# Attention row sums: which score tiles VectorE adds, and how its first addition is formed

## The reference

```python
q = _split_heads(x @ Wq + bq, h); k = _split_heads(x @ Wk + bk, h); v = _split_heads(x @ Wv + bv, h)
pattern = einsum('bhid,bhjd->bhij', k, q) * scale
prob = softmax(pattern, axis=-2)
out = einsum('bhis,bhid->bhsd', prob, v)
out.transpose(0, 2, 1, 3).reshape(b, s, h * dv) @ Wo + bo
```

## Time and profile before

| | |
|---|---|
| median of 3 runs | 4653.44 us (4646.86 to 4657.02) |
| the profiled execution | 4646.07 us |
| its span, first to last instruction | 4644.1 us |
| granted TensorE clock, mean | 0.977 |
| busy: PE, DVE, ACT, POOL | 4351.6, 3295.5, 2175.5, 2707.8 us |
| VectorE's copies into acc_d (L1178) | 64, median 1004 ns |
| VectorE's additions into acc_d (L1176) | 128, median 1537 ns |
| GpSimd's additions (L770) | 704 and 64 firsts, 2512 and 2386 ns mean |

### The profile page before, as it was taken

How to read it: one execution, slowest core, us unless ns; L and a number is a source line. 1 busy time by engine, 2 the same in 40 slices (tenths; PEclk the granted TensorE clock), 3 DMA queues, 4 the chain that set the end, 5 groups by cost and what they waited for, 6 DMA issues and landing times.

```text
span 4644.1 us, 67290 instructions
## 1 busy us (share of the span) xinstructions
PE 4351.6 (94%) x25496; PEld 2560.7 (55%) x25496; DVE 3295.5 (71%) x4434; ACT 2175.5 (47%) x3523; POOL 2707.8 (58%) x1205
## 2 busy tenths in 40 slices
PE   7999999999999999999999999858999897999898
PEld 5445454554554545545545545426777665777665
DVE  6777877777777777777787787476666455666455
ACT  5445444444444444444444444315666443666442
POOL 2867767667666676676676776804454332454332
PEclk8999999999999999999999999979999998999999
DMA  2000000000000000000000000010000100000001
GB/s 79 6 11 13 8 11 5 16 11 6 11 15 6 11 6 16 11 5 11 15 6 11 13 8 7 1 59 1 1 1 0 38 1 19 1 1 1 1 1 37
DMA packets 81401, 55.73 MB, mean 12 GB/s; under 512 B 48532, under 2 KB 71016, under 8 KB 81128
## 3 DMA queue, kind: packets, MB, share of 16 engines
q1 hardware_dynamic: 81128, 51.92, 4.2%
HBM read 30.66 MB, written 4.19 MB: 8 GB/s over the span
## 4 chain that ended last, share of the span: by engine, by line
PE 44%; POOL 25%; issue 12%; DVE 11%; ACT 7%; POOLq 1%; DMA 1%; SPq 0%; DVEq 0%; ACTq 0%
POOL accp L770 21%; PE psum L1521 8%; PE psum L1533 8%; PE psum L1668 5%; PE psum L1488 4%; PE psum L1798 2%; PE psum L1714 2%; PE psum L1728 2%; ACT lp L967 2%; POOL accp L766 2%; PE psum L1811 2%; DVE accd L1176 2%; PE psum L1465 2%; PE psum L1705 2%; PE psum L1473 1%
## 5 line engine op out<-in xcount | busy, mean ns | idle before, releaser
L770 POOL TENSOR_TENSOR accp<-accp,prob 128x1024 f32<-128x1024 f32 x704 | 1768.6, 2512 | 492.2 <-ACT prob L921 414.2
L921 ACT ACTIVATE prob<-psum 128x1024 f32<-128x1024 f32 x1024 | 1020.5, 1025 | 1462.7 <-PE psum L1521 1374.6
L1153 DVE TENSOR_REDUCE mx<-psum 128x1 f32<-128x512 f32 x1984 | 1277.2, 685 | 347.3 <-PE psum L1488 298.8
L1533 PE MATMUL psum<-prob,vv 128*64 128x512 f32 x4096 | 992.9, 606 | 0.0
L1488 PE MATMUL psum<-kh,qh 64*128 64x512 f32 x2048 | 492.2, 470 | 56.7 <-DVE mx L1153 48.6
L1533 PEld LDWEIGHTS psum<-prob,vv 128*64 128x64 f32 x4096 | 248.6, 136 | 490.1 <-issue 420.4
L787 POOL TENSOR_TENSOR lp<-lp,lrcp 128x1024 f32<-128x1024 f32 x128 | 242.6, 1895 | 451.7 <-DVE lrcp L1293 451.7
L1488 PEld LDWEIGHTS psum<-kh,qh 64*128 64x128 f32 x2048 | 205.0, 184 | 522.9 <-DVE mx L1153 442.2
L1521 PE MATMUL psum<-nm,one 64*128 64x512 f32 x2048 | 429.1, 408 | 14.1 <-ACT prob L921 6.5
L1521 PE MATMUL psum<-qh,kh 64*128 64x512 f32 x2048 | 412.3, 391 | 0.0
L1521 PE MATMUL psum<-qh,kl 64*128 64x512 f32 x2048 | 412.0, 391 | 0.0
(11 more groups left out here) (197 smaller groups left out, 6797.3 us busy)
## 6 DMA issues: line engine op xcount, KB each, us to landing
kl<-kl SPq DMA_DIRECT2D x64, 256.0 KB, 3.8
wqk<-L_attn_Wq SPq DMA_DIRECT2D x64, 64.0 KB, 2.1
rot_l<-const_rot SPq DMA_DIRECT2D x2, 2048.0 KB, 9.0
out<-lpT SPq DMA_DIRECT2D x32, 128.0 KB, 1.7
wqkv_l<-L_ffn_wqkv SPq DMA_DIRECT2D x4, 768.0 KB, 10.4
w_l<-L_ffn_w SPq DMA_DIRECT2D x4, 618.0 KB
wqk<-L_attn_Wk SPq DMA_DIRECT2D x32, 64.0 KB, 2.0
wv_p<-L_attn_Wv SPq DMA_DIRECT2D x16, 128.0 KB, 2.3
```

The lines of the kernel that those rows point to most:

```text
L770: pool.tensor_tensor(acc_p[cp][:], first[:], prob[kt % PRING][:], ALU.add).then_inc(pool_sum, 1)
L921: act.activation(prob[t % PRING][:], psum[:, S_BANK + 2 * (t % 2):S_BANK + 2 * (t % 2) + 2, :].rearrange("p a b -> p (a b)"), ACT.Exp, sca ...
L1153: dve.tensor_reduce(mx4[:, e, qt, c:c + 1], ps, AX_X, ALU.max).then_inc(ring_free, 1)
L1533: mm = pe.matmul(psum[j * DH:(j + 1) * DH, O_BANK, :], vv[:, kt, s * DH:(s + 1) * DH], prob[t % PRING][:, j * T:(j + 1) * T], start=(kt == ...
```

## The change

Each half gets its own set of three tiles for VectorE: tiles 8, 9 and 12 in the first half, 2, 3 and 10 in the second, in place of 3, 7 and 11 in both. The first two of a set are neighbours, and one addition `prob + prob` into `acc_d` takes both; the copy that started `acc_d` is gone. GpSimd still takes 13 tiles and makes 12 additions and one join per half, with other tile numbers. The waits of ScalarE and the counts of the semaphores follow. The places of the maxima are the same.

```diff
-SUM_DVE = (3, 7, 11)
-SUM_POOL = tuple(k for k in range(KT) if k not in SUM_DVE)
+SUM_DVE = ((8, 9, 12), (2, 3, 10))
+SUM_POOL = tuple(tuple(k for k in range(KT) if k not in tiles) for tiles in SUM_DVE)
 JOIN = -1
-POOL_SEQ = SUM_POOL[1:-1] + (JOIN,) + SUM_POOL[-1:]
-POOL_OPS = len(POOL_SEQ)
-DVE_OPS = len(SUM_DVE)
+POOL_SEQ = tuple(tiles[1:-1] + (JOIN,) + tiles[-1:] for tiles in SUM_POOL)
+POOL_OPS = len(POOL_SEQ[0])
+DVE_OPS = len(SUM_DVE[0]) - 1
...
+        def dve_used(cp, kt):
+            return max(SUM_DVE[cp].index(kt), 1)
...
-                    if kt in SUM_DVE:
-                        act.wait_ge(dve_sum, G * (CP * DVE_OPS) + OFF_DVE + cp * DVE_OPS + SUM_DVE.index(kt) + 1)
+                    if kt in SUM_DVE[cp % CP]:
+                        act.wait_ge(dve_sum, G * (CP * DVE_OPS) + OFF_DVE + cp * DVE_OPS + dve_used(cp % CP, kt))
...
             def add_sum(G, cp, j):
-                kt = SUM_DVE[j]
-                dve.wait_ge(exp_done, G * STEPS + cp * KT + kt + 1)
-                if j:
-                    dve.wait_ge(dve_sum, G * (CP * DVE_OPS) + OFF_DVE + cp * DVE_OPS + j)
-                    dve.tensor_tensor(acc_d[cp][:], acc_d[cp][:], prob[kt % PRING][:], ALU.add).then_inc(dve_sum, 1)
-                else:
-                    dve.tensor_copy(acc_d[cp][:], prob[kt % PRING][:]).then_inc(dve_sum, 1)
+                tiles = SUM_DVE[cp]
+                dve.wait_ge(exp_done, G * STEPS + cp * KT + tiles[j] + 1)
+                left = prob[tiles[0] % PRING]
+                if j > 1:
+                    dve.wait_ge(dve_sum, G * (CP * DVE_OPS) + OFF_DVE + cp * DVE_OPS + j - 1)
+                    left = acc_d[cp]
+                dve.tensor_tensor(acc_d[cp][:], left[:], prob[tiles[j] % PRING][:], ALU.add).then_inc(dve_sum, 1)
...
-                            if kt in SUM_DVE:
-                                add_sum(G, cp, SUM_DVE.index(kt))
+                            if kt in SUM_DVE[cp][1:]:
+                                add_sum(G, cp, SUM_DVE[cp].index(kt))
```

More of the change, by code:

```diff
@@ L407, in adaln_block, with pool_used @@
         OFF_S, OFF_POOL, OFF_DVE, OFF_RING = STEPS, CP * POOL_OPS, CP * DVE_OPS, RING_PAIR
-        def pool_used(kt):
-            return 1 if kt == SUM_POOL[0] else POOL_SEQ.index(kt) + 1
+        def pool_used(cp, kt):
+            return 1 if kt == SUM_POOL[cp][0] else POOL_SEQ[cp].index(kt) + 1
+        def dve_used(cp, kt):
+            return max(SUM_DVE[cp].index(kt), 1)
         def phase_end(eng, phase):
@@ L760, in head_sums @@
                 for cp in range(CP):
-                    for i, kt in enumerate(POOL_SEQ):
+                    for i, kt in enumerate(POOL_SEQ[cp]):
                         n = G * (CP * POOL_OPS) + OFF_POOL + cp * POOL_OPS + i
@@ L768, in head_sums @@
                         pool.wait_ge(exp_done, G * STEPS + cp * KT + kt + 1)
-                        first = acc_p[cp] if i else prob[SUM_POOL[0] % PRING]
+                        first = acc_p[cp] if i else prob[SUM_POOL[cp][0] % PRING]
                         pool.tensor_tensor(acc_p[cp][:], first[:], prob[kt % PRING][:], ALU.add).then_inc(pool_sum, 1)
@@ L916, in exps @@
                     cp, kt = divmod(t - PRING, KT)
-                    if kt in SUM_DVE:
-                        act.wait_ge(dve_sum, G * (CP * DVE_OPS) + OFF_DVE + cp * DVE_OPS + SUM_DVE.index(kt) + 1)
+                    if kt in SUM_DVE[cp % CP]:
+                        act.wait_ge(dve_sum, G * (CP * DVE_OPS) + OFF_DVE + cp * DVE_OPS + dve_used(cp % CP, kt))
                     else:
-                        act.wait_ge(pool_sum, G * (CP * POOL_OPS) + OFF_POOL + cp * POOL_OPS + pool_used(kt))
+                        act.wait_ge(pool_sum, G * (CP * POOL_OPS) + OFF_POOL + cp * POOL_OPS + pool_used(cp % CP, kt))
                     act.activation(prob[t % PRING][:], psum[:, S_BANK + 2 * (t % 2):S_BANK + 2 * (t % 2) + 2, :].rearrange("p a b -> p (a b)"),
```

## The result

The changed kernel takes 4656.07 us, the median of 20 runs (4652.66 to 4664.6). The kernel before, on the same chips, takes 4649.9 us (20 runs, 4643.42 to 4657.02). The ratio is 1.0015, with a 95% interval of 1.0009 to 1.0022: the change makes the kernel 4 to 10 us slower (the medians differ by 6.2), about the 0.2% from which the prediction counted a difference. The prediction was 4660 us, with +7.2 us for the step from one kernel to the other and a forecast of 0 to +15 us. The profiled execution took 4657.56 us, with a span of 4655.6 us and a granted clock of 0.974 (before: 4646.07, 4644.1, 0.977).

What follows compares the result with a forecast made beforehand. TensorE's own work plus some 4 us of stalls was taken to bound each pair. Ordinary pairs +5.2, second-type heads elsewhere +2.9, last pair's first head -0.57 and last head -0.3 gave +7.2 us: 4660 us, range 4636 to 4680.

Steps and rivals of the forecast that it cites:

- additions of groups 4 and 6 in second heads: First half of second heads: additions wait for GpSimd's running operation; reductions come late, stalling TensorE 1.05 and 1.06 us.
- the race: First head, group 4: VectorE's addition comes 0.12 us behind GpSimd's start and waits it out, a stall of 1.64 us.
- The middle sum: Both heads: without the addition behind the middle sum, TensorE's wait for VectorE there goes, 1.14 us per head.
- the operations of the first half: Old copy of group 1, additions of groups 3 and 5: cost 1.82 us in a first head, nothing in a second.
- the terms named for faster: Chances of a faster kernel: half of the won race's 0.12, idle GpSimd 0.06, 0.01 of the forecast; given as 0.16.
- A pair: Ordinary pair of heads, 13 of them: first head -0.57, second head +0.97, together +0.40 us, in all +5.2.
- the last pair: Its first head was forecast at -0.57 us, its last head at -0.3.
- the pair that turns the second batch: One head like a second head, +0.97 us; its first head between -1.6 and +1.6, taken as 0.
- the last head: No maxima there, GpSimd sets the end: between -1.5 and +1.1 us, taken as -0.3.
- VectorE wins the race: Rival, first head's group 4: VectorE's addition starts before GpSimd's tile 11, saving 24 us, to 4636; chance 0.12.
- the additions find GpSimd idle everywhere: Rival: VectorE's additions never wait for GpSimd, about 56 us faster, 4597 us; chance 0.06.
- the additions of group 9: Second half: addition in the old copy's place makes reductions late, 0.37 us of stall in first heads, nothing in second heads.

Runs made afterwards that it cites:

- e4_pool_holds: Changed kernel, but GpSimd starts tiles 10 and 14 of the first half only after VectorE's addition, and does its join last: 4596.02 us, ratio 0.9884 to the kernel before.
- e5_race: Changed kernel plus a tiny GpSimd operation ahead of its addition of tile 11 in the first half: 4630.28 us, ratio 0.9955 to the kernel before.
- e6_groups_3_5: Changed kernel, but VectorE takes tiles 6, 7 and 10 in the first half instead of 8, 9 and 12: 4609.34 us, ratio 0.9912 to the kernel before.
- e1_second_half: Kernel before with only the second half changed (tiles 2, 3 and 10, no copy); first half keeps 3, 7, 11 and the copy: 4623.71 us, ratio 0.9944.
- e10_join_last: Changed kernel, but GpSimd adds VectorE's sum in after its last tile, with no wait: 4659.41 us, ratio 1.0022 to the kernel before.
- e3_copy_kept: Changed tiles, but the first of each set is copied into `acc_d` and the second added: 4855.55 us, ratio 1.0447 to the kernel before.
- e11_hold_one: `e4_pool_holds` without the wait at tile 14, so GpSimd is held at tile 10 alone: 4637.42 us, ratio 0.9974 to the kernel before.

## Why the prediction was right

**The mechanism held in its numbers.** The additions of groups 4 and 6 in second heads ended 1.08 us behind GpSimd, the reductions came 4.48 us after the exponential, and the second head lost 2.04 us to its middle sum for 2.11 forecast. The first head lost the race by 0.11 us, for 0.12, and came out at +0.45 for +0.57. `e4_pool_holds` and `e5_race` leave the groups, the tiles and the kind of addition as they are and change only when GpSimd starts; the stalls go, so it is the meeting with GpSimd that makes them. The first head of `e6_groups_3_5` shows the other factor, the number of couples behind.

**The middle sum.** It gave 1.18 and 1.15 us for 1.14, with no wait of ScalarE for GpSimd in its place. In `e1_second_half` the second half is changed alone: 0.9944.

**What was argued and not needed, and a sum that is off.** The prediction says that the operations of the first half cost nothing in a second head before the change because a group of two couples follows. The rows have a simpler reason: they met little of GpSimd (the additions took 1.52 and 1.53 us, where 1.21 is the time with GpSimd idle), so they came only some 0.3 us late. The cost of nothing was right. And the chances do not add up as written: the terms named for faster give 0.13 (0.06, 0.06 and 0.01), for the same 0.48, for slower 0.39, not 0.16, 0.47 and 0.37; the range doesn't hang on it.

**The parts where the size was off.** A pair came to +0.16 us, not +0.40: 3.1 us less over 13 pairs. Three terms that I took as 0 or as a gain were off the other way: the last pair came to +0.8 where the forecast had -0.9, and the pair that turns the second batch to +2.25. The last pair's first head took 66.02 us to its middle sum for 63.94, +2.08 where +0.57 was forecast. TensorE there:

```profile
2894.45 0.50 PE L1492 MATMUL psum<-kh,qh 64*128 64x512 f32 x2 [1.58 <-DVE mx L1157]
...
2896.35 3.48 PE L1537 MATMUL psum<-prob,vv 128*64 128x512 f32 x8
```

It is the same stall as in the other first heads, but the eight products behind it took 3.48 us, not the 1.94 of the earlier trace rows. The windows show the granted clock:

```profile
2892.00:2894.00 2.00, 0.87 (x8) 0.38 (x4) 2.00 (x2) 0.19 (x1) 0.62 (x1) 1.00 0.00 0
2894.00:2896.00 2.00, 1.55 (x12) 1.19 (x12) 1.91 (x4) 0.92 (x2) 0.00 (x0) 1.00 0.00 0
2896.00:2898.00 2.00, 2.00 (x6) 0.53 (x7) 1.56 (x3) 0.94 (x1) 0.99 (x1) 0.52 0.00 0
```

A fall to the level of 1.2 GHz behind a stall was in no term of my sum. Whether it made the kernel longer is open: in `e10_join_last`, where the clock stayed up, this stretch took 64.37 us, but the whole last pair took 167.19 us, for 167.18 here. The pair that turns the second batch had +0.97 in the forecast (its first head taken as 0), and the last head gained nothing for -0.3. Of the 1.3 us more of the pair that turns the second batch, 0.8 are in its first head behind the middle sum (36.63 us for 35.82), where the granted clock falls before the change too, but after it for longer: in windows of 2 us it reads 0.58, 0.50, 0.50 and 0.72, before 0.82, 0.50 and 0.83. In `e10_join_last` the stretch took 35.82. Counted over the trace, from the first reciprocal (156.68, now 162.41) to the last (3016.86, now 3027.18), the change costs 4.6 us, and the first head 1.9 more: 6.5 us for the +7.2 predicted. The two profiled spans differ by 11.5 us. Of the rest, 3.8 lie ahead of the first score (100.70 and 104.49 us), where the change does nothing, and 1.2 behind the last reciprocal. So the total was right partly by luck: the errors of the pairs and of the three odd places cancelled.

**The rivals.** That VectorE wins the race was priced at 24 us; `e5_race`, which makes it win, gains 25.8. That the additions find GpSimd idle everywhere was priced at 4597 us; `e4_pool_holds`, which makes GpSimd idle at the two places of the first half, takes 4596.0. The first price held. The second agrees closer than its terms do: it counted the additions of group 9 as freed too, which `e4_pool_holds` leaves waiting (about 0.35 us a pair), and took off 0.6 us a pair for additions that don't quite fit. The conditions just don't arise by themselves.

## What to carry to other kernels

Where a two-input VectorE addition and GpSimd both read SBUF, as here, the addition's cost is less in its own 1.2 us than in what GpSimd has just begun. Here, taking neighbouring tiles from GpSimd made it idle, and an idle GpSimd started its next tile just ahead of the addition. Before moving such an operation, look for GpSimd's start beside it and for what is queued behind it: a place where GpSimd is nearly through or that has slack behind it, or a wait on the engine that has time to spare, was worth about 1.2% here, while 115 us less VectorE work alone was worth nothing. And a hold at one place moves the held engine's later operations: two holds gained 60 us, a third gave 22 back, and one hold alone gained 19.

## What the runs showed of the hardware that I had not expected

- Between two VectorE operations in direct succession, a waiting GpSimd operation gets in: in `e3_copy_kept` the copy and the addition each waited for one GpSimd operation, 1.57 and 3.18 us.
- TensorE's granted clock fell to the level of 1.2 GHz behind some stalls of under 2 us, and not behind others of the same length. In the changed kernel the stall of a first head's group 4 (waits of 1.58 us) left the clock at 1.00 in the ordinary pairs and took it to 0.52 in the last pair, where the work behind took 1.5 us longer. In `e11_hold_one` the same stall in second heads let it fall in some pairs and not in others. What tells them apart was not settled.
